# Expert weights for each token fetched by broadcast transfers instead of a matmul, and weight preparation moved into neighbouring stages

## Chip, cores and metric

The kernel runs on one core of a Trainium2 chip. The metric is the device time of one execution in microseconds (us). The core has a matmul engine (PE, with its weight loads PEld shown apart), a vector engine (DVE), an activation engine (ACT), a general engine (POOL), a queue that issues transfers (SP) and 16 DMA engines behind it.

## What is computed

A residual stream x of 4 x 256 tokens by 256 channels goes through four pairs of an attention-like layer and a feed-forward layer, each added with a tanh gate. The change touches layer 0's feed-forward, a mixture of 64 experts of width 64 with 4 chosen per token, and two shared ones of width 256:

```
logits = flat @ router_w                      # 1024 tokens x 64 experts
comb   = softmax scores of the top 4, normed; zero for other experts
g, u   = silu(flat @ wg[e]), flat @ wu[e]
routed = sum over e of comb[:, e] * (g * u) @ wd[e]
shared = the same with swg, swu, swd, and no comb
```

After it come layer 1's attention over the context (l1x), layer 1's feed-forward with an attention of its own (l1f), layer 2 with a feed-forward on weights rounded to -1, 0 and 1 (the rounding needs the mean of |w| over each whole weight), and layer 3. Those later layers need the weights Wq, Wk, Wv, Wc, W_in, W_up, W_down and the two rounded ones turned, 128 x 128 block by block.

## The kernel before

Each engine runs its own program, and semaphores order them. The stretch that matters has five parts.

**Start.** Layer 0's attention and the router. DVE's `chosen(h)` makes the combination weights of 512 tokens (h is 0 or 1) into `ct2`, twice side by side (line 2060). PE turns them (line 731), ACT copies them as rounded high parts to `comb` (`combine_high`), and DVE's `combine_low` puts the rest into the lower 64 partitions (line 2068).

**Routed experts.** Two experts make a pair, so 128 hidden rows fill the partitions; 32 pairs are 8 turns of a hardware loop with four slots `wraw`. A unit u is one pair and one half of the tokens: 64 units. PE runs `up(u+1)` (12 matmuls of 128x512: gate, then up, each in three high/low products), then one matmul `pick` x `comb` (line 769) that spreads the pair's weights over the partitions into a bank, then `down(u)` (6 matmuls, line 778). ACT makes `sg` (silu), DVE `hu` (line 2104) and `hh = bank * hu` (line 2108), ACT `hhi`, DVE `hlo` (line 2096), and `down(u)` waits for `hlo`. POOL splits each pair's raw weights into high and low (`split`, lines 2701 and 2704), and copies `pick`. SP loads the pair four ahead as soon as POOL has freed its slot (five transfers, 384 KB, lines 562 and 564).

**Shared experts.** Four more pairs (8 units) without weights. SP loads the two layer-2 weights `l2_raw` just ahead of them.

**Preparation.** When the experts are done, ACT copies `yT`, PE turns it and DVE adds it to `xs` (line 2125). Only then SP loads `stage` 0 to 3 and `wo`; ACT takes the sums of |w| (line 1602), PE adds them up (line 822), DVE rounds in six passes (lines 2133 to 2135) and makes the statistics of `xs` (from line 1974); PE turns 36 groups of blocks (lines 834 and 836) and ACT copies them out (line 1520), after the rounding is done. A last product `wa` (line 843) ends it, and everybody waits for it.

**Attention A.** 24 groups in slots written out by hand. In the first slots (-3 to -1) the pipeline fills: ACT `norm` (line 1684), POOL parts, PE turns, DVE maxima, ACT `mT`, a small transfer `qT<-mT`, and from slot 0 on `by_key`.

Of the kernel before, what the change touches and what calls it, by code (L numbers as in the profile page):

```python
# [8 lines left out]
P = 128  # L9
ALU = mybir.AluOpType  # L10
# [15 lines left out]
R = 16  # L26
# [114 lines left out]
def maxima_landed(stream, s):  # L141
# [6 lines left out]
     "router_ps", "router_max", "router_exp", "comb", "comb_ps", "comb_high", "comb_low", "x_split"),  # L148
# [11 lines left out]
    ("",) * 24 + ("pick_ready", "weights_high", "weights_split", "downs_split", "gate_made", "up_made", "gate_used",  # L160
                  "hidden_full", "hidden_high", "hidden_made", "up_used", "weight_made", "hidden_used", "experts_out", "y_rows",
# [31 lines left out]
def flamingo(nc, I, out):  # L193
    with ExitStack() as ctx:
        sems, batch_sems = {}, []

# [22 lines left out]
        def sb(name, shape, dt=F32):  # L219
# [64 lines left out]
        comb = sb("comb", [P, TOKENS], FR)  # L284
        picks = sb("picks", [P, E // 2, P], BF16)
        pick = [sb(f"pick{k}", [P, P], FR) for k in range(2)]
# [16 lines left out]
        First = namedtuple("First", "c cT kvT kv xn xT oT tmp lg lb lr cb ct ct2 m8 bn mv ve rs least st")  # L303
# [4 lines left out]
                       ct=sb(f"ct0{h}", [P, T0, E]), ct2=sb(f"ct2{h}", [P, T0, 2, E]), m8=sb(f"m8{h}", [P, T0, 8]),  # L308
# [20 lines left out]
        top[0] = region  # L329
        top[0] += DC * TOKENS * 4  # L330
        stage = [sb(f"stage{k}", [P, 2048]) for k in range(4)]
        wo = sb("wo", [P, DC, D])
        after_prep = max(top[0], after_experts + 8192)
        top[0] = region
        tern = [sb(f"tern{k}", [P, 2048], BF16) for k in range(2)]
# [43 lines left out]
        rc = sb("rc", [P, 16])  # L379
        at_f = sb("at_f", [P, B, NT, D])  # L380

# [131 lines left out]
        FIRST_STAGES = len(PREP)  # L513
# [3 lines left out]
        PREPB += blocks_of(tern[1], D, F1, lambda ic, o, n: w2qT[:, ic, o:o + n])  # L517

# [18 lines left out]
        def _(sp):  # L537
# [53 lines left out]
            sp.wait_ge(once("picks"), 2)  # L591
# [6 lines left out]
            sp.wait_ge(once("hidden_used"), 2 * PAIRS + 4)  # L598
            sp.wait_ge(once("experts_out"), 2 * HALVES)
# [7 lines left out]
            stg = once("stage_rest_loaded")  # L607
# [54 lines left out]
        def _(pe):  # L662
# [61 lines left out]
            def turn_combine(h):  # L724

                t = first[h]
                pe.wait_ge(S("comb"), h + 1)
                if h > 0:
                    pe.wait_ge(S("comb_low"), h)
                for i in range(T0):  # L730
                    last = pe.transpose(bank[7][:, i * P:(i + 1) * P], t.ct2[:, i, :, :], ident[:, :])
                last.then_inc(S("comb_ps"), 1)
# [14 lines left out]
            def up(k, h, u, pair, shared=False):  # L747

                n = 3 * (2 * k + h)
# [42 lines left out]
            pe.wait_ge(S("comb_low"), HALVES)  # L792
# [11 lines left out]
            for u in range(2 * SLOTN):  # L804
                if u + 1 < 2 * SLOTN:
                    up((u + 1) // 2, (u + 1) % 2, T * 8 + u + 1, T * SLOTN + (u + 1) // 2, shared=True)
                down(u // 2, u % 2, T * 8 + u, T * SLOTN + u // 2, last_pair=u // 2 == SLOTN - 1)

# [11 lines left out]
            pe.wait_ge(once("xs_updated"), 4)  # L820
            pe.wait_ge(once("abs_sums"), 2)
            mm(bank[4][:, 0:2], ones[:, :], st[:, 0:2], start=True, stop=True).then_inc(once("abs_total"), 1)

            pe.wait_ge(once("stage_loaded"), 5 * 16)
            for g, (srcs, dst) in enumerate(PREP + PREPB):
                if g >= 4:
                    pe.wait_ge(once("prep_done"), g - 3)
                if g == FIRST_STAGES:
                    pe.wait_ge(once("stage_rest_loaded"), 3 * 16)
                if g == len(PREP):  # L830
                    pe.wait_ge(once("ternary"), 2)
                for j, src in enumerate(srcs):
                    if g < len(PREP):
                        last = pe.transpose(bank[g % 4][:, j * P:(j + 1) * P], src, ident[:, :])
                    else:
                        last = pe.transpose(bankb[g % 4][:, j * P:(j + 1) * P], src, identb[:, :])
                last.then_inc(once("prep_made"), 1)

            g = len(PREP + PREPB)
            pe.wait_ge(once("prep_done"), g - 3)  # L840
            for m in range(DC):
                for cc in range(DC):
                    last = mm(bank[g % 4][:, m * R:(m + 1) * R], wo[:, cc, m * P:(m + 1) * P], am[:, cc, :],
                              start=cc == 0, stop=cc == DC - 1)
            last.then_inc(once("wa_made"), 1)
            pe.wait_ge(once("prepared"), 1)
            pe.wait_ge(once("prep_done"), len(PREP + PREPB))
# [146 lines left out]
            def attention(stream):  # L994
# [111 lines left out]
                def by_key(s, k):  # L1106
# [4 lines left out]
                    if stream == "C" and n == 0:  # L1111
                        pe.wait_ge(S("l2_pre"), 16)
                    if k == 0:
# [113 lines left out]
                for sl in range(-3, S_ + (1 if stream == "A" else 3)):  # L1227
                    here = lambda what: standing_there(stream, what, sl)
                    for k in range(8):
# [47 lines left out]
                        for s in here("by_query"):  # L1277
# [240 lines left out]
        def _(act):  # L1518
# [42 lines left out]
            def combine_high(h):  # L1561

                act.wait_ge(S("comb_ps"), h + 1)
                copy(comb[:, T0 * P * h:T0 * P * (h + 1)], bank[7][:, :]).then_inc(S("comb_high"), 1)
# [16 lines left out]
            def gate(k, u):  # L1581
                n = 3 * k
# [7 lines left out]
            with act.Fori(0, PAIRS // SLOTN) as t:  # L1590
                for k in range(2 * SLOTN):
                    gate(k, t * 8 + k)
            act.wait_ge(once("batch_cleared"), 1)
# [5 lines left out]
            act.wait_ge(once("l2_loaded"), 2 * 16)  # L1599

            for k, scratch in enumerate((w1qT, w2qT)):
                act.activation(scratch[:, :, :].rearrange("p c f -> p (c f)"), l2_raw[k][:, :], ACT.Abs, accum_out=st[:, k:k + 1]).then_inc(once("abs_sums"), 1)
            for g, (srcs, dst) in enumerate(PREP + PREPB):
                if g == 0:
                    act.wait_ge(once("ternary"), 2)
                act.wait_ge(once("prep_made"), g + 1)
                src = (bank if g < len(PREP) else bankb)[g % 4]
                copy(dst, src[:, 0:len(srcs) * P], scale=0.25 if g < DC else 1.0).then_inc(once("prep_done"), 1)

# [58 lines left out]
            def attention(stream):  # L1668
# [55 lines left out]
                for sl in range(-3, S_ + (2 if stream == "A" else 3)):  # L1724
                    here = lambda what: standing_there(stream, what, sl)
                    for k in range(8):
                        for s in here("by_key"):
# [58 lines left out]
            act.wait_ge(once("prepared"), 1)  # L1786
# [1127 lines left out]
```

## Time and profile before

| what | us |
|---|---|
| median of 3 runs | 1261.07 (1260.91 to 1263.65) |
| the profiled execution | 1259.72 |
| its span in the profile | 1257.9 |
| routed experts, first to last unit | about 87 to 369 |
| shared experts | about 369 to 405 |
| preparation, until attention A's first `norm` | 405 to 435.6 |

The profile gives for each engine what it did and what ended its waits. PE's clock is granted in two levels, 1.00 (2.4 GHz) and 0.50 (1.2 GHz). A share of DMA is that of 16 engines' time.

### The profile page before, as it was taken

To read this page: it belongs to the slowest core of one execution; us is meant where nothing else is said; L and a number is where in the kernel's file an instruction comes from. 1 tells how busy PE (TensorE), PEld (TensorE's weight loads), DVE (VectorE), ACT (ScalarE), POOL (GpSimd) and SP (SyncE) were. 2 spreads that over 40 slices of the span, in tenths; PEclk is the share of its full clock that TensorE was granted. 3 is DMA by queue.
4 is the path that set the end of the run, shared out by engine and by line. 5 is a ranking of instruction groups with operands and counts; after the bars stand their busy time and mean duration, and the time that the engine had idled before them with its cause. 6 is when DMAs were issued, how large, how long until landed. Compare 5 with 4: busy or idle time off the path is not lost.

```text
span 1257.9 us, 18978 instructions
## 1 busy us (share of the span) xinstructions
PE 1044.5 (83%) x6622; PEld 667.9 (53%) x6625; DVE 742.0 (59%) x1684; ACT 524.7 (42%) x883; POOL 328.0 (26%) x626
## 2 busy tenths in 40 slices
PE   4369999999998688877988899991464878999997
PEld 2258888888887432333455435650322434566575
DVE  6875554444443577787565212479697674784743
ACT  1223233333333556565554430233473553544543
POOL 7023434343333456435343200001310300000000
PEclk9659999999999768999999899795686799999999
DMA  6101121111310400000000300002000000000000
GB/s 151 42 1 39 38 50 42 46 46 42 117 25 1 142 2 2 2 3 2 3 3 4 118 1 1 1 1 51 1 2 1 3 2 1 1 9 1 9 10 9
DMA packets 62444, 32.09 MB, mean 26 GB/s; under 512 B 47104, under 2 KB 61072, under 8 KB 62112
## 3 DMA queue, kind: packets, MB, share of 16 engines
q1 hardware_dynamic: 62368, 31.10, 9.3%
q8 instruction: 45, 0.74, 0.2%
q14 instruction: 31, 0.25, 0.1%
HBM read 29.64 MB, written 1.05 MB: 24 GB/s over the span
## 4 chain that ended last, share of the span: by engine, by line
PE 69%; DVE 21%; ACT 4%; issue 3%; POOL 1%; DMA 1%; SPq 0%; POOLq 0%; DVEq 0%; ACTq 0%; PEldq 0%
PE bank L762 16%; PE bank L778 8%; PE bank L874 4%; PE bank L1160 3%; DVE mx L2272 3%; PE bank L989 2%; PE bank L1341 2%; PE bank L957 2%; PE bank L1358 2%; PE bank L919 2%; PE bank L1343 2%; PE bank L1092 2%; PE bank L1140 2%; PE bank L1193 1%; DVE mxc L2272 1%
## 5 line engine op out<-in xcount | busy, mean ns | idle before, releaser
L2272 DVE TENSOR_REDUCE mx<-bank 128x2 f32<-128x512 f32 (+1 forms) x176 | 117.7, 689 | 71.0 <-PE bank L1092 35.1
L1708 ACT ACTIVATE prob<-bank 128x512 f32<-128x512 f32 x176 | 102.9, 597 | 89.3 <-PE bank L1140 62.1
L1520 ACT ACTIVATE hhi<-hh 128x512 fp32r<-128x512 f32 x72 | 45.5, 632 | 153.1 <-DVE hh L2108 140.4
L2104 DVE TENSOR_TENSOR hu<-bank,sg 128x512 f32<-128x512 f32 x64 | 44.3, 692 | 97.1 <-PE bank L762 97.1
L762 PE MATMUL bank<-xh,wh 128*128 128x512 f32 x288 | 91.6, 399 | 0.0
L762 PE MATMUL bank<-xh,wl 128*128 128x512 f32 x288 | 90.5, 395 | 0.0
L762 PE MATMUL bank<-xlo,wh 128*128 128x512 f32 x288 | 90.1, 394 | 0.0
L2096 DVE TENSOR_TENSOR hlo<-hh,hhi 128x512 fp32r<-128x512 f32 x72 | 57.2, 794 | 50.7 <-ACT hhi L1520 50.7
L2704 POOL TENSOR_TENSOR wl<-wraw,wh 128x512 fp32r<-128x512 f32 x72 | 80.6, 1119 | 13.0 <-POOL wh L2701 13.0
L1585 ACT ACTIVATE sg<-bank 128x512 f32<-128x512 f32 x72 | 43.1, 598 | 61.9 <-PE bank L762 61.9
L762 PEld LDWEIGHTS bank<-xh,wh 128*128 128x128 f32 x288 | 54.6, 190 | 13.3 <-issue 0.3
L762 PEld LDWEIGHTS bank<-xlo,wh 128*128 128x128 f32 x288 | 54.3, 188 | 13.4
L762 PEld LDWEIGHTS bank<-xh,wl 128*128 128x128 f32 x288 | 54.4, 189 | 12.4
L874 PE MATMUL bank<-mun,xT 128*128 128x512 f32 x128 | 59.2, 607 | 1.2 <-ACT xw L1520 1.1
L778 PE MATMUL bank<-hhi,wh 128*128 128x512 f32 x144 | 56.8, 394 | 0.9 <-DVE hlo L2096 0.9
L778 PE MATMUL bank<-hhi,wl 128*128 128x512 f32 x144 | 56.9, 395 | 0.0
L1092 PE MATMUL bank<-kTx,qT 48*128 48x256 bf16 x256 | 51.0, 308 | 6.3 <-DVE kTx L2236 5.6
L778 PE MATMUL bank<-hlo,wh 128*128 128x512 f32 x144 | 56.1, 390 | 0.0
L2701 POOL CAST wh<-wraw 128x512 fp32r<-128x512 f32 x72 | 37.7, 523 | 64.1 <-PE bank L762 44.4
L1140 PE MATMUL bank<-qT,kTx 51*128 51x512 bf16 x128 | 51.2, 419 | 2.5 <-ACT prob L1708 2.5
L1708 ACT ACTIVATE probc<-bank 128x512 f32<-128x512 f32 x64 | 36.8, 596 | 36.1 <-PE bank L1140 35.7
L2272 DVE TENSOR_REDUCE mxc<-bank 128x2 f32<-128x512 f32 x64 | 41.4, 686 | 15.9 <-PE bank L1092 14.5
(456 smaller groups left out, 2275.0 us busy)
## 6 DMA issues: line engine op xcount, KB each, us to landing
wraw<-in_L_ffn_wg_dram SPq DMA_DIRECT2D x64, 64.0 KB, 2.3
wraw<-in_L_ffn_wu_dram SPq DMA_DIRECT2D x64, 64.0 KB, 2.4
wraw<-in_L_ffn_wd_dram SPq DMA_DIRECT2D x32, 128.0 KB, 2.4
l_raw<-in_L_ffn_w_dram SPq DMA_DIRECT2D x2, 1024.0 KB, 6.8
mun<-in_L_ffn_mu_dram SPq DMA_DIRECT2D x1, 2048.0 KB, 7.6
xs<-in_x_dram SPq DMA_DIRECT2D x1, 1024.0 KB, 5.5
w1s<-in_L_ffn_W_dram SPq DMA_DIRECT2D x2, 512.0 KB, 7.7
stage<-in_L_ffn_W_in_base_dram SPq DMA_DIRECT2D x1, 1024.0 KB, 7.8
```

What stands on the lines that cost most here:

```text
L762: last = mm(bank[4 + (n + m) % 4][:, :], w[k % 2][:, m, cc * P:(cc + 1) * P], v[:, cc, tok], start=j == 0 and cc == 0, stop=j == 2 and cc ...
L778: last = mm(bank[2 * m + h][:, :], w[k % 2][:, 2, m * P:(m + 1) * P], v[h][:, :], start=False, stop=last_pair and j == 2, skip_group_check ...
L874: last = mm(bank[n % 2][:, :], xT3[b % 2][:, cc, i * P:(i + 1) * P], mun[:, cc, ch * 512:(ch + 1) * 512], start=cc == 0, stop=cc == 1)
L1092: last = mm(to[:, f * N:(f + 1) * N], t.qT[rows, s % 4, u, i * P:(i + 1) * P], key_operand(L, b, s, 8 * g + 2 * j + f, rows, slice(0, N)), ...
L1140: last = mm(to[:, :], key_operand(L, b, s, 8 * g + 2 * j, rows, slice(ti * P, (ti + 1) * P)), t.qT[rows, s % 4, u:u + 2, :], start=True, s ...
L1520: return act.activation(dst, src, ACT.Copy, scale=scale)
L1585: act.activation(sg[k % 2][:, :], bank[4 + n % 4][:, :], ACT.Silu).then_inc(once("gate_used"), 1)
L1708: act.activation(t.prob[k][:, :], bank[3 + n % 2][:, :], ACT.Exp).then_inc(S("probs"), 1)
L2096: tt(hlo[k % 2][:, :], hh[k % 2][:, :], hhi[k % 2][:, :].bitcast(F32), ALU.subtract)\
L2104: tt(hu[k % 2][:, :], bank[4 + (n + 1) % 4][:, :], sg[k % 2][:, :], ALU.mult).then_inc(once("up_used"), 1)
L2272: V.reduce_max(out_, bank[n % 3][:, :].rearrange("p (h t) -> p h t", h=heads), AX, negate=True)\
L2704: G.tensor_tensor(low[:, cols, :], wraw[k][:, cols, :], high[:, cols, :].bitcast(F32), ALU.subtract)\
```

## The change

The selection product is gone. `comb` is now a plain [64 experts, 1024 tokens] tile; SP writes it once to `comb_rows` in device memory, and for each pair reads its two rows back, each spread over 64 partitions, into one of two `spread` tiles of 512 KB. The next transfer into a tile is issued when both `hh` of the pair that used it are done. DVE reads `spread` instead of a bank. The stage loads are issued while the shared experts run (their tiles lie elsewhere now), the sums of |w| and the rounding are placed between the shared units, and of the 36 turned groups only 12 stay ahead of the attention; 24 and `wa` go into its slots -4, -2 and -1.

```diff
@@ SP @@
+            def spread_weights(k, pair):
+                W(spread[k % 2][:, :], comb_rows.rearrange("(q e) t -> q e t", e=2)[pair].unsqueeze(1).broadcast_to([2, F, TOKENS]))\
+                    .then_inc(once(f"weights_spread{k % 2}"), 16)
...
+            sp.wait_ge(S("comb_high"), HALVES)
+            W(comb_rows, comb[:, :]).then_inc(once("comb_kept"), 16)
+            sp.wait_ge(once("comb_kept"), 16)
+            for k in range(2):
+                spread_weights(k, k)
+            end_of_batch(sp)
             with sp.Fori(0, E // 2 // SLOTN - 1) as t:
                 for k in range(SLOTN):
                     sp.wait_ge(once("downs_split"), t * SLOTN + (k + 1))
                     load_experts(k, t * SLOTN + (SLOTN + k), None)
+                    sp.wait_ge(once("hidden_full"), t * (2 * SLOTN) + (2 * k + 2))
+                    spread_weights(k, t * SLOTN + (k + 2))
+            for k in range(2):
+                sp.wait_ge(once("hidden_full"), E - 2 * SLOTN + 2 * k + 2)
+                spread_weights(k, E // 2 - 2 + k)
...
-            sp.wait_ge(once("hidden_used"), 2 * PAIRS + 4)
-            sp.wait_ge(once("experts_out"), 2 * HALVES)
+            sp.wait_ge(once("batch_arrived"), 4)
@@ PE @@
-                pe.wait_ge(once("up_used"), u + 2)
-                if not shared:
-                    if h == 0:
-                        pe.wait_ge(once("pick_ready"), pair + 1)
-                    mm(bank[4 + (n + 2) % 4][:, :], pick[k % 2][:, :], comb[:, tok], start=True, stop=True)\
-                        .then_inc(once("weight_made"), 1)
...
+                if u == 1:
+                    pe.wait_ge(once("abs_sums"), 2)
+                    mm(bank[6][:, 0:2], ones[:, :], st[:, 0:2], start=True, stop=True).then_inc(once("abs_total"), 1)
+                    pe.wait_ge(once("abs_total"), 2)
...
+            for g in PREP_AT["first"]:
+                prepare(g)
...
+                        if stream == "A":
+                            for g in PREP_AT.get((sl, k), ()):
+                                prepare(g)
@@ ACT, shared units @@
+                    act.activation(tern[k][:, :], l2_raw[k][:, :], ACT.Abs, accum_out=st[:, k:k + 1]).then_inc(once("abs_sums"), 1)
@@ DVE @@
-                    dve.wait_ge(once("weight_made"), u + 1)
+                    dve.wait_ge(once(f"weights_spread{k // 2 % 2}"), t * 32 + (16 * (k // 4) + 16))
-                    tt(hh[k % 2][:, :], bank[4 + (n + 2) % 4][:, :], hu[k % 2][:, :], ALU.mult).then_inc(once("hidden_full"), 1)
+                    tt(hh[k % 2][:, :], spread[k // 2 % 2][:, k % 2 * 512:(k % 2 + 1) * 512], hu[k % 2][:, :], ALU.mult)\
+                        .then_inc(once("hidden_full"), 1)
...
+                if k == 1:
+                    dve.wait_ge(once("abs_total"), 1)
+                    step(ts(wdq[:, :], bank[6][:, 0:2], 1.0 / (F1 * D), 1e-5, ALU.mult, ALU.max))
...
+                if k >= 2:
+                    w = l2_raw[(k - 2) // 3][:, :]
+                    if k in (2, 5):
+                        step(ts(w, w, st[:, 2 + k // 5:3 + k // 5], -1.0, ALU.mult, ALU.max))
...
+        PREP_BANKS = (3, 4, 5)
+        PREP_AT = {"first": range(12), (-4, 0): range(12, 16)}
+        for n in range(8):
+            PREP_AT[-2, n] = range(16 + n, 17 + n)
+            PREP_AT[-1, n] = range(24 + 2 * n, 26 + 2 * n) if n < 6 else range(30 + n, 31 + n)
```

POOL no longer copies `pick`, and it clears its tiles for the attention without waiting for the experts' end. DVE makes one `ct` where it made `ct2` twice, and `combine_low` is gone.

## Rows read from the trace of the kernel before

**Rows 1.** Windows, routed units: PE, PEld, DVE, ACT, POOL busy, PE clock, DMA share, GB/s

```profile
94.00:366.00 272.00, 272.00 (x1176) 220.32 (x1176) 135.50 (x187) 85.17 (x132) 107.86 (x154) 1.00 0.20 51
```

**Rows 2.** Chain that ended last: start, us, what

```profile
96.51 2.78 PE bank L762 x12
...
369.31 2.78 PE bank L762 x12
373.71 2.79 PE bank L762 x12
...
398.75 2.80 PE bank L762 x12
```

**Rows 3.** Timeline of one routed unit: start, us, engine, line [idle before]

```profile
342.06 0.69 DVE L2108 TENSOR_TENSOR hh<-bank,hu 128x512 f32<-128x512 f32 x1
...
343.45 0.69 DVE L2096 TENSOR_TENSOR hlo<-hh,hhi 128x512 fp32r<-128x512 f32 x1 [0.70 <-ACT hhi L1520]
...
345.76 0.39 PE L778 MATMUL bank<-hhi,wh 128*128 128x512 f32 x1
```

**Rows 4.** DMA view of 103 to 111.5 us, one pair's expert loads

```profile
q1 hardware_dynamic: 1232, 0.39, 20.3%
```

**Rows 5.** DMA view of 1124 to 1129 us, one output transfer, 128 partitions; last: KB, landing

```profile
DMA packets 272, 0.26 MB, mean 52 GB/s; under 512 B 16, under 2 KB 272, under 8 KB 272
...
q1 hardware_dynamic: 272, 0.26, 15.4%
...
out_dram<-xs SPq DMA_DIRECT2D x1, 256.0 KB, 2.2
```

**Rows 6.** DMA view of 452.4 to 452.8 us, one `qT<-mT`

```profile
DMA packets 15, 0.01 MB, mean 15 GB/s; under 512 B 3, under 2 KB 15, under 8 KB 15
```

**Rows 7.** Windows in large loads (last two: DMA share, GB/s)

```profile
715.00:718.00 3.00, 3.00 (x10) 1.46 (x9) 0.00 (x0) 1.70 (x3) 2.69 (x1) 0.50 1.02 354
709.00:713.00 4.00, 0.77 (x8) 0.51 (x6) 0.86 (x4) 0.60 (x1) 0.00 (x0) 0.84 0.89 358
```

**Rows 8.** Timeline of the start

```profile
76.39 2.12 DVE L2060 TENSOR_TENSOR ct<-ct,st 128x256 f32<-128x256 f32 x2
...
86.20 0.60 ACT L1520 ACTIVATE comb<-bank 128x512 fp32r<-128x512 f32 x1 [4.67 <-PE bank L731]
...
92.67 0.69 DVE L2108 TENSOR_TENSOR hh<-bank,hu 128x512 f32<-128x512 f32 x1
```

**Rows 9.** Timeline of POOL's split of one pair's gate and up weights

```profile
359.06 0.61 POOL L2701 CAST wh<-wraw 128x512 fp32r<-128x512 f32 x1 [0.91 <-PE bank L762]
...
359.85 1.30 POOL L2704 TENSOR_TENSOR wl<-wraw,wh 128x512 fp32r<-128x512 f32 x1 [0.18 <-POOL wh L2701]
```

**Rows 10.** Timeline of the preparation

```profile
405.57 2.06 ACT L1520 ACTIVATE yT<-bank 128x512 f32<-128x512 f32 x4 [2.52 <-PE bank L778]
...
408.89 3.23 DVE L2125 SCALAR_TENSOR_TENSOR xs<-bank,gates,xs 128x512 f32<-128x512 f32 x4 [5.12 <-PE bank L814]
...
420.71 2.70 DVE L1974 BATCH_NORM_STATS2 bn<-xs 128x6 f32<-128x256 f32 x8
420.83 1.98 ACT L1520 ACTIVATE wqkvT<-bank 128x256 f32<-128x256 f32 x6 [9.42 <-DVE tern L2135]
...
426.55 0.17 DVE L1979 SCALAR_TENSOR_TENSOR nmx<-mvx,rsx 128x8 f32<-128x8 f32 x1
...
435.61 1.09 ACT L1684 ACTIVATE xn<-xs,nmx,rsx 128x256 f32<-128x256 f32 x2 [0.69 <-DVEq L2141]
```

**Rows 11.** Windows of the preparation's last 24 groups, and of attention A's fill

```profile
426.40:435.00 8.60, 7.81 (x68) 5.32 (x66) 0.50 (x3) 8.52 (x25) 0.00 (x0) 1.00 0.00 0
436.00:454.00 18.00, 11.81 (x72) 6.04 (x72) 9.55 (x16) 5.93 (x9) 12.62 (x41) 0.50 0.01 2
```

**Rows 12.** Windows around the end of the experts

```profile
406.00:408.00 2.00, 0.22 (x2) 0.25 (x3) 0.00 (x0) 2.00 (x5) 1.94 (x2) 0.98 0.00 0
408.00:410.00 2.00, 2.00 (x11) 2.00 (x10) 1.09 (x2) 2.00 (x3) 1.83 (x5) 0.50 0.41 133
```

More of the change, by code:

```diff
@@ L283, in flamingo @@
         xh = sb("xh", [P, DC, TOKENS], FR)
-        comb = sb("comb", [P, TOKENS], FR)
-        picks = sb("picks", [P, E // 2, P], BF16)
-        pick = [sb(f"pick{k}", [P, P], FR) for k in range(2)]
+        comb = sb("comb", [E, TOKENS])
+        spread = [sb(f"spread{k}", [P, TOKENS]) for k in range(2)]
+        top[0] += 1024
         SLOTN = 4
@@ L728, in turn_combine @@
                 if h > 0:
-                    pe.wait_ge(S("comb_low"), h)
+                    pe.wait_ge(S("comb_high"), h)
                 for i in range(T0):
-                    last = pe.transpose(bank[7][:, i * P:(i + 1) * P], t.ct2[:, i, :, :], ident[:, :])
+                    last = pe.transpose(bank[7][0:E, i * P:(i + 1) * P], t.ct[:, i, :], ident[:, :])
                 last.then_inc(S("comb_ps"), 1)
@@ L745, in _, with up @@
             turn_combine(1)
-            def up(k, h, u, pair, shared=False):
-                n = 3 * (2 * k + h)
+            def up(k, h, u, pair):
+                n = 2 * (2 * k + h)
                 tok = slice(h * 512, (h + 1) * 512)
@@ L816, in _ @@
                 last.then_inc(once("y_rows"), 1)
[L820 to L829, printed above, removed]
+            pe.wait_ge(once("stage_loaded"), 8 * 16)
@@ L830, in _, with prepare @@
+            def prepare(g):
+                if g == 0:
+                    pe.wait_ge(once("xs_updated"), 4)
+                if g >= len(PREP_BANKS):
+                    pe.wait_ge(once("prep_done"), g + 1 - len(PREP_BANKS))
                 if g == len(PREP):
                     pe.wait_ge(once("ternary"), 2)
-                for j, src in enumerate(srcs):
+                if g == len(PREP + PREPB):
+                    for m in range(DC):
+                        for cc in range(DC):
+                            last = mm(bank[prep_bank(g)][:, m * R:(m + 1) * R], wo[:, cc, m * P:(m + 1) * P], am[:, cc, :],
+                                      start=cc == 0, stop=cc == DC - 1)
+                    last.then_inc(once("wa_made"), 1)
+                    return
+                for j, src in enumerate((PREP + PREPB)[g][0]):
@@ L840, in _ @@
[L840 to L847, printed above, removed]
+            for g in PREP_AT["first"]:
+                prepare(g)
@@ L1226, in attention @@
                 inside = lambda s: 0 <= s < S_
-                for sl in range(-3, S_ + (1 if stream == "A" else 3)):
+                for sl in range(-4, S_ + (1 if stream == "A" else 3)):
                     here = lambda what: standing_there(stream, what, sl)
@@ L1563, in combine_high @@
                 act.wait_ge(S("comb_ps"), h + 1)
-                copy(comb[:, T0 * P * h:T0 * P * (h + 1)], bank[7][:, :]).then_inc(S("comb_high"), 1)
+                copy(comb[:, T0 * P * h:T0 * P * (h + 1)], bank[7][0:E, :]).then_inc(S("comb_high"), 1)
             tokens_turned(0, 1, (6, 7))
@@ L1597, in _, with prepared @@
                     copy(yT[:, m, h * 512:(h + 1) * 512], bank[2 * m + h][:, :]).then_inc(once("experts_out"), 1)
[L1599 to L1605, printed above, removed]
+            act.wait_ge(once("ternary"), 2)
+            def prepared(g):
+                srcs, dst = (PREP + PREPB)[g]
                 act.wait_ge(once("prep_made"), g + 1)
-                src = (bank if g < len(PREP) else bankb)[g % 4]
+                src = (bank if g < len(PREP) else bankb)[prep_bank(g)]
                 copy(dst, src[:, 0:len(srcs) * P], scale=0.25 if g < DC else 1.0).then_inc(once("prep_done"), 1)
+            for g in PREP_AT["first"]:
+                prepared(g)
             def x_turned(b):
@@ L2059, in chosen @@
                 step(V.reciprocal(t.st[:, 4:8], t.st[:, 0:4]))
-                step(*[tt(t.ct2[:, :, k, :], t.ct[:, :, :], t.st[:, 4:8].unsqueeze(2).broadcast_to([P, T0, E]), ALU.mult)
-                       for k in range(2)])
+                step(tt(t.ct[:, :, :], t.ct[:, :, :], t.st[:, 4:8].unsqueeze(2).broadcast_to([P, T0, E]), ALU.mult))
                 dve.sem_inc(S("comb"), 1)
-            def combine_low(h):
-                dve.wait_ge(S("comb_high"), h + 1)
-                low = comb[E:2 * E, T0 * P * h:T0 * P * (h + 1)]
-                tt(low, bank[7][E:2 * E, :], low.bitcast(F32), ALU.subtract).then_inc(S("comb_low"), 1)
             norm0(0)
```

101 lines of the change are left out of this document (50 added, 51 removed).

## The prediction, on record before the result was known

> **What bounds the kernel now.** I read the windows first, to see which engine is full where: over the routed experts PE is busy all 272 us, at full clock, while DVE has half of it and the others less [rows 1]. The chain of waits says the same: from 96.51 to 369.31 us it is nothing but PE, one block of twelve matmuls per unit, 62 units in 272.80 us, so 4.40 us a unit; the shared units, which have no selection product, come every (398.75 - 373.71) / 6 = 4.17 us [rows 2]. The timeline of one unit shows that nobody else is close: `hlo` ends at 344.14 and the `down` that needs it starts at 345.76, 1.6 us of slack [rows 3]. After the experts the chain leaves PE. ACT ends its `yT` copies at 407.63, makes its sums, and then stands idle for 9.42 us until DVE's rounding is through; the first of the 36 copies starts at 420.83 and attention A's first `norm` at 435.61 [rows 10]. So two things are for sale: 0.23 us in each routed unit, and the 30 us between the experts and the attention.
>
> **Routed units: what goes.** The product costs PE 4.40 - 4.17 = 0.226 us a unit. The last one stands in the block at 369.31, since that is still 4.40 us ahead of the next. From the unit at 96.51 to the one at 373.71 it is 63 times: 14.2 us off, if PE stays the bound [rows 2]. `hh` reads `spread` instead of a bank; `hlo` already has both sources outside the banks, at the same 0.69 us [rows 3]. POOL's `pick` copies go too, on an engine with slack.
>
> **Routed units: what comes.** For each pair a transfer of 512 KB must land before the pair's first `hh`. Tile k is free when pair q's two `hh` are done, and pair q+2 wants it three units later less the stretch from the start of `up` to `hh`: about 4.2 + 4.2 + 2.8 = 11 us. That is the price at which PE starts to wait. What does the transfer take? Two facts decide.
>
> First, one engine's speed. In the window at 709 us the 16 engines moved 1.43 MB in 0.89 x 4.00 x 16 = 57 engine-us: 25.1 GB/s per engine; at 715 us, in which broadcast rows of 4 KB were read, 1.06 MB in 49 engine-us: 21.7 [rows 7].
>
> Second, how many engines take part. The output transfer from 128 partitions has 256 packets of 1 KB and 16 records below 512 B, one closing record for each engine [rows 5]. A `qT<-mT`, which goes from 12 partitions to 3, has 12 packets of 512 B and only 3 closing records [rows 6]: it ran on 3 engines, the count of its smaller outermost dimension. The new transfer's source is [2 experts][64 copies][1024 tokens]; the copies have no step in memory and can't be merged with the experts, so its outermost dimension is 2. By the reading of rows 6 it runs on 2 engines. Each moves 262 KB: 10.4 us at 25.1 GB/s, 12.1 at 21.7. I take 10.4, as the other engines are idle meanwhile.
>
> On the page "DMA: Bandwidth & Descriptors" (rules for kernel authors) the Trainium skill says the same against this change: a leading zero-stride broadcast of c copies, or any outermost dimension below 16, "confines the whole DMA to at most c engines". Rows 6 agree, with 3 closing records for the side of 3. By that page's specification of some 27 GiB/s an engine, an estimate, the 262 KB would take 9 us rather than 10.4.
>
> These two engines also carry their sixteenth of the expert loads: 20.3% of 8.5 us = 1.7 us a pair [rows 4]. So the two engines are busy 10.4 + 1.7 = 12.1 us for each pair, against 8.35 us that PE needs. Then it is no longer a matter of slack: throughput binds, whatever the order. The tile is asked for again about 3.6 us after it has landed (`hh`, `hhi`, `hlo`, `hu` and the second `hh`, four steps of 0.69 on DVE and one of some 0.7 on ACT, [rows 3]), while the other tile's transfer is still running, so that the queue of these two engines never empties. The forecast is one pair every 12.1 us.
>
> **Start.** `comb` is ready at 86.8 us [rows 8]. One of two `ct2` products in each half goes (1.06 of the 2.12 us that the first pair took), and PE's second turn no longer stands behind `combine_low(0)`; I take 1.4 us earlier in all, 85.4 (0.5 to 2). The write of 256 KB has the shape of the output transfer, 2.2 us [rows 5], so 87.6. Of those 2.2, 0.8 (15.4% of 5 us) are its packets and 1.4 the rest. The first spread lands at 87.6 + 1.4 + 10.4 = 99.4 (the first `hh` was at 92.67), the second at 109.8. 28 pairs follow with a load beside them, and two without: 109.8 + 28 x 12.1 + 2 x 10.4 = 469.4 for pair 31.
>
> **Into the shared units.** SP issues the 2 MB of `l2_raw` and the first shared load behind the last spread. On the two engines they come after it: 131 KB each, 5.2 us, and 1.7; then 1.4 of landing and 2.1 for POOL's split (0.61, a gap and 1.30, [rows 9]). The first shared `up` starts at 469.4 + 10.4 = 479.8. Without this wait PE would be there at 469.4 + 3.6; the wait costs 6. The next unit is at 484.0 and was at 373.71: 110.3 later. ACT's sums lie under that wait. The rounding takes DVE one pass of 1.2 to 1.4 us a unit, in some 2 us of idle time; I count nothing (0 to 1). At the second shared unit PE stops for a tiny product and DVE's answer: I estimate 0.9 us from small DVE steps of 0.17 [rows 10] and three hand-overs (0.5 to 1.5). Sum at the experts' end: +111.2.
>
> **Preparation.** It starts with the loads landed, the rounding done, and POOL ready. What is left ahead of `norm`: DVE's statistics, 6.0 us (420.71 to 426.72) from 412.12, so 418.2; and 12 groups, which took ACT from 420.83 to 426.4, 5.6 us [rows 10, 11], up to 8 if PE is at half clock. I take 419.3 against 435.61: 16.3 us off. The other 24 groups were 8.52 us of ACT and 7.81 us of PE at full clock; they go into a fill of 18 us in which ACT was busy 5.93 and PE 11.81 at half clock [rows 11]. Twice 7.81 and 11.81 is 27, 9 more than the fill; at full clock it is 1.6 more. In slot -1 eight groups stand ahead of ACT's `mT`, which the first `by_key` waits for. I take 5 (1 to 9). Net -11.3, bounds -15 to -7.
>
> **Sum.** 1257.9 + 111.2 - 11.3 = 1357.8 of span; the profiled execution took 1.8 more than its span and the median 1.35 more than that: 1361, and I say 1360.
>
> **Rivals.**
> *A: all 16 engines take part* (chance 0.12). For it: every large transfer of this trace did so; the only evidence for fewer is of small transfers between partitions, none from device memory. Then 512 KB are some 1.3 us of packets, landing in about 3, far below 11; the first `hh` comes near the old time (I take 0.6 us earlier). 1257.9 - 0.6 - 14.2 + 0.9 - 11.3 = 1232.7, some 1236 by the median. It decides at about 3 engines: with 4 the pair's load on an engine is 5.2 + 1.7 = 6.9, below 8.35, and the kernel is faster.
> *B: two engines, and the clock falls besides* (0.04). PE idles 3.7 us a pair. After the experts PE was nearly idle for two microseconds, and the clock went from 0.98 to 0.50 [rows 12]. At half clock a pair's matmuls take up to 16.7 us. If half of the pairs' time goes that way, a pair takes about 14.4 and the kernel 1361 + 30 x 2.3 = 1430. Against it: 1.5 us a pair are to spare before PE's work sets the pace again, and a short drop fits in.
> *C: two engines, but a pair costs less*, since the loads' packets slip between those of the spread or if one engine alone is faster than any window here shows (0.02): 10.4 a pair, 1361 - 28 x 1.7 = 1313.
> That nothing changes (0.02) would need errors that cancel.
>
> **How the numbers follow.** 0.80 for the forecast in its bounds: a pair from 11.2 us (half of the loads hidden) to 13.2 (the speed two thirds of the way to 21.7 GB/s) is 30 x -0.9 to 30 x +1.1 around 1361, 1334 to 1394, and the fill adds 4 on either side: 1330 to 1398. A, B and C are outside. Slower: forecast, B, C, 0.86. This kernel's measurement can tell 0.2%, or 2.5 us, from no change: same 0.02, faster 0.12.
>
> **What would show it.** In the profile after, the DMA view of one spread should have 128 packets of 4 KB and 2 closing records, and its landing some 12 us or more; `hh` should be released by `spread`'s DMA; the chain should step in pairs of 12 us with DMA in it; the DMA share in that stretch about 0.3 in spite of full queues. If instead there are 16 closing records, A is right and all from "routed units: what comes" to the shared wait falls. `norm` of attention A should follow the `xs` update by some 7 us instead of 23. Wrong would make me: an engine that reads 4 KB rows much faster or slower when alone, or a fill that swallows the groups or stalls on each.

## Result: 7% slower, and the profile after

The changed kernel takes 1349.6 us (median of 4 runs, 1347.46 to 1351.17), the kernel before 1262.4 in the same comparison: a ratio of 1.070, with an interval of 1.067 to 1.072. The forecast was 1360 in a range of 1330 to 1398.

| what | before | after |
|---|---|---|
| span of the profiled execution | 1257.9 | 1349.4 |
| first `hh` | 92.67 | 98.61 |
| first `hh` of the shared units | 372.19 | 470.13 |
| `yT`, the experts' end | 405.57 | 504.34 |
| attention A's first `norm` | 435.61 | 516.50 |
| attention A's first `prob` | 454.71 | 546.91 |

Read down, the difference is 5.9 us at the first `hh`, 97.9 at the end of the routed experts, 98.8 at `yT`, 80.9 at `norm`, 92.2 at `prob`, and 91.5 at the end. So the whole loss is made in the 32 pairs, where (470.13 - 98.61) / 32 = 11.61 us pass per pair. The last of these 32 steps is longer than the others, since it holds the stop ahead of the shared units: 14.14 us, from pair 31's first `hh` at 455.99, where the 31 steps before it take 11.53 us each. The new preparation takes 17.9 us off ahead of `norm`, and the fill of the attention's pipeline gives 11.3 of them back.

The windows show the routed stretch and the fill (columns as in [rows 1]):

```profile
100.00:450.00 350.00, 285.19 (x1088) 221.01 (x1089) 139.68 (x184) 80.49 (x129) 100.73 (x118) 0.91 0.25 79
516.50:546.90 30.40, 25.76 (x147) 14.05 (x145) 12.55 (x19) 15.96 (x34) 13.33 (x44) 0.59 0.00 1
```

PE, full before, is now idle for 65 of 350 us. The DMA share is 0.25, so three quarters of the 16 engines' time is free while everybody waits for transfers. What they wait for is in the view of waits (waiter <- releaser: us in total, times, longest):

```profile
DVE hh L2136 <- DMA spread<-comb_rows: 105.6, 32, 10.8
...
PE bank L799 <- DVE hlo L2124: 77.3, 31, 10.9
```

Once per pair `hh` waits for its spread, and PE for `hlo` behind it. The DMA view from 88 to 96 us, between the first spread's issue and its landing, shows how many engines carry it:

```profile
DMA packets 102, 0.42 MB, mean 52 GB/s; under 512 B 0, under 2 KB 0, under 8 KB 102
...
q1 hardware_dynamic: 102, 0.42, 12.7%
```

Nothing but packets of 4 KB, and 12.7% of 16 engines is 2.03 engines: two are busy all the time, at 26 GB/s each, and fourteen do nothing. The loads of the next experts were issued meanwhile, and none of their packets runs in these 8 us. The timeline of SP tells why:

```profile
82.83 0.56 SPq L605 DMA_DIRECT2D comb_rows<-comb  x1
85.81 1.26 SPq L585 DMA_DIRECT2D spread<-comb_rows  x2
87.62 10.18 SPq L574 DMA_DIRECT2D wraw<-in_L_ffn_wg_dram  x2
```

The two spreads are issued in 1.26 us; the two small loads behind them take SP 10.18 us to issue. They are held while the two busy engines work through the spreads. Therefore the longest pieces that the chain of waits has in the loop, where one would look first, name SP and not the spread:

```profile
82.83 2.97 DMA comb_rows<-comb
87.62 7.82 SPq L574
123.51 5.14 SPq L576
169.94 5.08 SPq L576
```

From 100 to 450 us SP's issues hold over four fifths of the chain (54.2% on line 574, 24.9% on 576, 5.2% on 585), and the spreads' transfers 4.2%, all of it in one piece of 14.78 us at 418.54, near the loop's end. Whether SP is the cause or only where the cause shows is a question for an experiment (the run with ACT's queue, below).

### The profile page after: what moved, and what is told of

Its sections match the earlier page's. It is cut to its first block, busy times and chain, and to the rows that moved or that the text cites. A ratio compares the mean times of both kernels' runs of the same rounds, so it can differ in the third digit from the quotient of the medians.

```text
span 1349.4 us, 18872 instructions
## 1 busy us (share of the span) xinstructions
PE 1067.5 (79%) x6560; PEld 672.3 (50%) x6560; DVE 743.7 (55%) x1680; ACT 520.9 (39%) x882; POOL 310.8 (23%) x591
## 4 chain that ended last, share of the span: by engine, by line
PE 45%; SPq 25%; DVE 18%; issue 5%; ACT 3%; DMA 2%; POOL 2%; POOLq 0%; DVEq 0%; ACTq 0%; PEldq 0%
SPq L574 15%; SPq L576 6%; PE bank L896 4%; PE bank L1185 3%; PE bank L1114 2%; PE bank L1011 2%; PE bank L1369 2%; PE bank L979 2%; PE bank L1386 2%; PE bank L941 2%; DVE mx L2302 2%; PE bank L1371 2%; PE bank L1165 2%; PE bank L790 1%; SPq L585 1%
## 5 line engine op out<-in xcount | busy, mean ns | idle before, releaser
L799 PE MATMUL bank<-hhi,wh 128*128 128x512 f32 x144 | 64.7, 449 | 77.3 <-DVE hlo L2124 77.3
L2136 DVE TENSOR_TENSOR hh<-spread,hu 128x512 f32<-128x512 f32 x64 | 50.7, 793 | 106.7 <-DMA spread<-comb_rows 105.6
L790 PE MATMUL bank<-xh,wh 128*128 128x512 f32 x288 | 99.7, 430 | 5.1 <-POOL wl L2728 4.8
L790 PE MATMUL bank<-xlo,wh 128*128 128x512 f32 x288 | 95.6, 415 | 0.0
L790 PE MATMUL bank<-xh,wl 128*128 128x512 f32 x288 | 94.0, 408 | 0.0
L799 PEld LDWEIGHTS bank<-hhi,wh 128*128 128x128 f32 x144 | 28.6, 199 | 96.2 <-DVE hlo L2124 62.6
L790 PEld LDWEIGHTS bank<-xh,wh 128*128 128x128 f32 x288 | 60.0, 209 | 20.7 <-POOL wl L2728 5.2
L790 PEld LDWEIGHTS bank<-xlo,wh 128*128 128x128 f32 x288 | 59.0, 205 | 15.0
L799 PE MATMUL bank<-hlo,wh 128*128 128x512 f32 x144 | 61.7, 428 | 0.0
L799 PE MATMUL bank<-hhi,wl 128*128 128x512 f32 x144 | 61.1, 424 | 0.0
```

What stands on the lines that cost most here:

```text
L790: last = mm(bank[4 + (n + m) % 4][:, :], w[k % 2][:, m, cc * P:(cc + 1) * P], v[:, cc, tok], start=j == 0 and cc == 0, stop=j == 2 and cc ...
L799: last = mm(bank[2 * m + h][:, :], w[k % 2][:, 2, m * P:(m + 1) * P], v[h][:, :], start=False, stop=last_pair and j == 2, skip_group_check ...
L2136: tt(hh[k % 2][:, :], spread[k // 2 % 2][:, k % 2 * 512:(k % 2 + 1) * 512], hu[k % 2][:, :], ALU.mult)\
```

## Experiments

### The same bytes on 16 engines, and on 4

The edit that matters most changes neither bytes nor rows, only the shape of the source. One transfer per expert, so that its outermost dimension is the 64 copies:

```diff
-                W(spread[k % 2][:, :], comb_rows.rearrange("(q e) t -> q e t", e=2)[pair].unsqueeze(1).broadcast_to([2, F, TOKENS]))\
-                    .then_inc(once(f"weights_spread{k % 2}"), 16)
+                for e in range(2):
+                    W(spread[k % 2][e * F:(e + 1) * F, :],
+                      comb_rows.rearrange("(q e) t -> q e t", e=2)[pair, e:e + 1, :].broadcast_to([F, TOKENS]))\
+                        .then_inc(once(f"weights_spread{k % 2}"), 16)
...
-                    dve.wait_ge(once(f"weights_spread{k // 2 % 2}"), t * 32 + (16 * (k // 4) + 16))
+                    dve.wait_ge(once(f"weights_spread{k // 2 % 2}"), t * 64 + (32 * (k // 4) + 32))
```

> Changed: the changed kernel, with each pair's spread transfer issued as two, one for each expert. The source of each is 64 copies of one row, so its outermost dimension is 64 where it was 2; bytes, rows and addresses are the same. Theory (two engines carry each spread, and their throughput sets the pair): all 16 engines take part, 33 KB each, and PE bounds the routed experts again: a pair every 8.4 us, no wait of hh for spread after the first, a median near 1262.4 - 0.6 - 14.2 + 0.8 - 6.6 = 1242 us (start, selection products, rounding beside the shared units, and what the new preparation took off by the trace of the changed kernel). Rival 1 (512 KB a pair, or 64 reads of the same row of device memory, is too much whatever engines carry it): pairs of about 11.6 us and 1350 us, as in the changed kernel. Rival 2 (what delays is SP, which issues the next transfer only when the queue has taken the last one): SP issues more now, 7 where it issued 6 per pair, and the median stays above 1300 us.

Measured: 1234.5 us (1230.3 to 1239.2), ratio to before 0.980 (0.976 to 0.984), so 115 us less than the changed kernel and faster than the kernel before. The window of its routed pairs:

```profile
100.00:350.00 250.00, 250.00 (x1080) 202.32 (x1079) 148.62 (x180) 82.99 (x127) 99.95 (x118) 1.00 0.45 113
```

PE is busy all 250 us at full clock. Its first `hh` starts at 90.40 and the first one of the shared units at 359.30: 8.40 us a pair. The waits and the DMA view from 200 to 233.6 us (last two columns: KB, us from issue to landing):

```profile
  DMA spread<-comb_rows: 3.0, 1
```

```profile
spread<-comb_rows SPq DMA_DIRECT2D x8, 256.0 KB, 3.9
```

One wait of 3.0 us, for the very first spread, and 3.9 us from issue to landing. Both rivals fall: neither the bytes nor the repeated reads of one row are too much, and SP issues one transfer more per pair without harm.

The second edit keeps the rows twice in device memory and leaves one transfer per pair, with a source of four rows of 32 copies:

```diff
-        comb_rows = nc.dram_tensor("comb_rows", (E, TOKENS), F32).ap()
+        comb_rows = nc.dram_tensor("comb_rows", (E, 2, TOKENS), F32).ap()
...
-                W(spread[k % 2][:, :], comb_rows.rearrange("(q e) t -> q e t", e=2)[pair].unsqueeze(1).broadcast_to([2, F, TOKENS]))\
+                W(spread[k % 2][:, :],
+                  comb_rows.rearrange("(q e) c t -> q (e c) t", e=2)[pair].unsqueeze(1).broadcast_to([4, F // 2, TOKENS]))\
...
-            W(comb_rows, comb[:, :]).then_inc(once("comb_kept"), 16)
-            sp.wait_ge(once("comb_kept"), 16)
+            for c in range(2):
+                W(comb_rows[:, c, :], comb[:, :]).then_inc(once("comb_kept"), 16)
+            sp.wait_ge(once("comb_kept"), 32)
```

> Changed: the changed kernel, with the rows kept twice in device memory (one more transfer of 256 KB at the start), so that the source of a spread is 4 rows of 32 copies each. Same bytes per pair, four engines where there were two. Theory (two engines' throughput): 131 KB an engine, 42 engine-us a pair over 4 engines is 5.3 us, with 1.1 us of expert loads 6.4 us, below the 8.35 us of PE: PE is the bound, and the time is within 3 us of that with 16 engines, some 1243 us. Rival (total bytes, or SP's issues): 1350 us, or somewhere between.

Measured: 1251.1 us (1245.7 to 1254.4), ratio 0.992 (0.988 to 0.995). (The 42 engine-us a pair in the expectation should read 21, a quarter of 84.3; its 5.3 us is worked out from 21.) In the loop the theory holds: 8.49 us a pair, and only the first `hh` waits for a spread. But the total is 17 us above the run with 16 engines, not 3. The two profiled executions are 19.9 us apart, and their traces say where: the first `hh` is at 100.14 in place of 90.40, the last pair's step takes 11.37 us in place of 8.43, since PE waits for the first shared weights, and the fill of attention A, from the first `norm` to the first `prob`, takes 30.8 us in place of 22.8. The first has two parts. `comb` was finished 3.8 us later, in a stretch that the edit does not touch. Then comes the chain's

```profile
86.91 3.63 DMA comb_rows<-comb
90.56 9.56 DMA spread<-comb_rows
```

where the run with 16 engines had 2.98 and 4.36, another 5.9 us. The fill is PE's clock, which two more windows show, first those with four engines, then with 16:

```profile
418.40:449.20 30.80, 25.78 (x139) 14.27 (x140) 12.77 (x20) 15.94 (x34) 13.29 (x44) 0.55 0.00 1
```

```profile
404.90:427.70 22.80, 16.95 (x139) 10.40 (x140) 12.67 (x20) 15.56 (x33) 13.05 (x43) 0.93 0.01 2
```

The same 139 matmul records, a granted clock of 0.55 against 0.93, 8.8 us more of PE's time and 8.0 us more of everybody's. In the expectation I had counted the fill as a constant; it has two values.

### Less in each spread, still on two engines

```diff
-                W(spread[k % 2][:, :], comb_rows.rearrange("(q e) t -> q e t", e=2)[pair].unsqueeze(1).broadcast_to([2, F, TOKENS]))\
+                W(spread[k % 2][:, 0:768], comb_rows.rearrange("(q e) t -> q e t", e=2)[pair, :, 0:768].unsqueeze(1).broadcast_to([2, F, 768]))\
...
-                    tt(hh[k % 2][:, :], spread[k // 2 % 2][:, k % 2 * 512:(k % 2 + 1) * 512], hu[k % 2][:, :], ALU.mult)\
+                    tt(hh[k % 2][:, :], spread[k // 2 % 2][:, k % 2 * 256:k % 2 * 256 + 512], hu[k % 2][:, :], ALU.mult)\
```

> Changed: the changed kernel, with only 768 of the 1024 tokens in each spread (packets of 3 KB for 4 KB, still two engines); the second half of the tokens is multiplied by the weights of tokens 256 to 767, so the output is that of other weights. Theory (two engines' throughput, near its threshold): 84.3 engine-us in four pairs is 10.5 us a pair and engine, three quarters are 7.9, with 1.0 to 1.7 us of expert loads 8.9 to 9.6 us a pair, still just above PE: 1350 - 31 x (11.57 - 9.25) = 1278 us, 1268 to 1288. Rival (a transfer costs by packet, not by byte: 128 packets as before): little less than 1350. Rival (latency of a chain from hh to the next spread, not throughput, sets the pair): a gain of 2.6 us a pair at most, and hh still waits for spread with the two engines idle for a part of each pair.

Measured: 1275.4 us (1274.0 to 1281.4). A pair takes (396.35 - 99.43) / 32 = 9.28 us, and its waits have the same form as with full spreads, at half the size:

```profile
DVE hh L2136 <- DMA spread<-comb_rows: 50.1, 29, 7.5
```

The second dose has 512 tokens (`0:512` in all four places, and both halves of the tokens read the same columns):

> Changed: the changed kernel, with only 512 of the 1024 tokens in each spread (packets of 2 KB, two engines); both halves of the tokens are multiplied by the weights of tokens 0 to 511, so the output is that of other weights. With 1024 tokens a pair took 11.61 us (hh of unit 0 to hh of unit 64, by 32), with 768 of them 9.28, so 2.33 us a quarter. Theory (throughput, below its threshold): 11.61 - 2 x 2.33 = 6.95 us an engine, less than PE's 8.35: PE is the bound, hh waits for spread only at the start, 8.4 to 8.5 us a pair as with 4 and 16 engines, and a median of 1235 to 1252 us, which that run's clock at the start and in the fill decides. Rival (the expert loads behind the spreads come late even so): hh, or PE by its weights, still waits in each pair, and the time lies at 1255 to 1275.

Measured: 1242.6 us (1238.9 to 1247.4), and (366.29 - 96.52) / 32 = 8.43 us a pair:

```profile
100.00:350.00 250.00, 250.00 (x1072) 202.19 (x1072) 146.77 (x178) 82.32 (x126) 99.81 (x118) 0.99 0.28 77
```

PE is full. Side by side, with KB (of 1000 bytes) for each of the engines that take part, and the pair once over all 32 steps and once over the 31 ahead of the last:

| tokens, engines | KB an engine | us a pair, 32 steps | 31 steps | median us |
|---|---|---|---|---|
| 1024, 2 | 262 | 11.61 | 11.53 | 1349.6 |
| 768, 2 | 197 | 9.28 | 9.12 | 1275.4 |
| 512, 2 | 131 | 8.43 | 8.39 | 1242.6 |
| 1024, 4 | 131 | 8.49 | 8.39 | 1251.1 |
| 1024, 16 | 33 | 8.40 | 8.40 | 1234.5 |

From 262 to 197 KB the pair follows the bytes, 2.41 us for 65.5 KB, which is 27 GB/s; below, it rests on PE. Rows three and four have the same bytes per engine and the same pair, although one moves twice as many bytes in all. The threshold lies between 131 and 197 KB an engine; the prediction put it at about 3 engines, which is 175 KB.

### Is SP the cause?

The spreads from pair 2 on go to ACT's queue, and SP has nothing but the loads of the experts in the loop:

```diff
-                    sp.wait_ge(once("hidden_full"), t * (2 * SLOTN) + (2 * k + 2))
-                    spread_weights(k, t * SLOTN + (k + 2))
...
+            act.wait_ge(once("comb_kept"), 16)
+            with act.Fori(0, E // 2 // SLOTN - 1) as t:
                 for k in range(2 * SLOTN):
                     gate(k, t * 8 + k)
+                    if k % 2 == 1:
+                        spread_weights(k // 2, t * SLOTN + (k // 2 + 2))
+            for k in range(2 * SLOTN):
+                gate(k, E - 2 * SLOTN + k)
+                if k in (1, 3):
+                    spread_weights(k // 2, E // 2 - 2 + k // 2)
```

> Changed: the changed kernel, with the spread transfers from pair 2 on issued by ACT's own queue, right behind hhi of the pair that used the tile, where SP issued them. SP's queue has the expert loads alone. The transfers themselves are as before, two outermost rows of 64 copies. Theory (the throughput of two DMA engines): the chain of waits named SP (21% of the span in its issues of expert loads), but SP was held up only because the queue behind it was full of spreads; without it a pair still takes 11.3 to 11.6 us and the median stays at 1340 to 1352 us. Rival (the blocked issues on SP are a cost of their own, since the next spread stands behind them): with the queue free of them a pair falls to the 10.5 us that a spread occupies an engine, or below, and the median to 1315 us or less.

Measured: 1349.8 us (1347.7 to 1353.0), ratio 1.070 like the changed kernel's, and (468.69 - 99.99) / 32 = 11.52 us a pair. The rival falls: the next spread no longer stands behind the loads' issues, and the pair stays as long. `hh` still waits for the spread, and one blocked issue can be seen on the new queue, the first of its 30 (the others took 0.54 us at most):

```profile
103.92 5.70 ACTq L1612 DMA_DIRECT2D spread<-comb_rows  x1
```

SP's share in the chain was where the two engines' backlog surfaced, not a cost of its own. One part of the expectation is wrong, though: SP was not held up only by spreads in its own queue. With none in it from pair 2 on, a load's issue between 100 and 345 us still takes 2.14 us on average, against 1.95 in the changed kernel and 0.58 with 16 engines, and lines 574 and 576 still have 15.5% and 4.4% of the whole chain. What these issues share with the spreads is the two busy engines.

### The preparation alone

The transfers' part is undone (product, `picks` and `combine_low` are back; in the shared units the banks go by two a unit), and the preparation's part stays:

```diff
-                    dve.wait_ge(once(f"weights_spread{k // 2 % 2}"), t * 32 + (16 * (k // 4) + 16))
+                    dve.wait_ge(once("weight_made"), u + 1)
...
-                    tt(hh[k % 2][:, :], spread[k // 2 % 2][:, k % 2 * 512:(k % 2 + 1) * 512], hu[k % 2][:, :], ALU.mult)\
+                    tt(hh[k % 2][:, :], bank[4 + (n + 2) % 4][:, :], hu[k % 2][:, :], ALU.mult)\
```

> Changed: the part on the preparation alone. The selection product, its picks and the low part of comb are as in the kernel before; the stage loads, sums, rounding and the 36 groups are where the changed kernel has them. Theory (sum of the changed kernel's own trace: 17.75 us off until the first norm, 11.2 us given back by the pipeline's fill with 24 groups and wa in it, 0.8 us in the shared units): 1262.4 - 17.75 + 11.2 + 0.8 = 1256.6 us, 1253 to 1259. Rival (the fill costs no more than the 5 us that was forecast, and the rest of the 11.2 us comes from the late transfers): 1250 us. Rival (the preparation saves nothing once the experts aren't delayed, since the stage loads then come later against them): 1262.

Measured: 1247.7 us (1247.6 to 1252.5), ratio 0.992 (0.989 to 0.995), 11.3 us faster than before where I expected 5.8. Its `norm` is at 418.15, 17.5 us earlier, as expected. The difference is the fill, 22.8 us where the changed kernel had 30.4. Here it is, and below it that of the kernel before:

```profile
418.15:440.98 22.83, 16.98 (x139) 10.44 (x140) 12.67 (x20) 15.58 (x34) 13.11 (x44) 0.93 0.01 1
```

```profile
435.60:454.70 19.10, 12.45 (x75) 6.18 (x76) 10.25 (x17) 6.79 (x9) 12.62 (x41) 0.50 0.01 2
```

Again a granted clock of 0.93 and the same 139 records. Against the 19.1 us of before, which ran at a clock of 0.50, the changed fill costs 3.7 us at the high clock and 11.3 at the low one. So the 3.7 is a net figure: the placement's cost, less what the faster clock gives back. The rival's 1250 is nearer than my sum, though its reason is not the one found: from `yT` to the first `prob` no engine waits for a transfer, here or there.

### Where the 24 groups stand

Both kernels below have 16 engines for the spreads. The first turns all 36 groups ahead of the attention:

```diff
-        PREP_AT = {"first": range(12), (-4, 0): range(12, 16)}
-        for n in range(8):
-            PREP_AT[-2, n] = range(16 + n, 17 + n)
-            PREP_AT[-1, n] = range(24 + 2 * n, 26 + 2 * n) if n < 6 else range(30 + n, 31 + n)
...
+        PREP_AT = {"first": range(36), (-1, 6): range(36, 37)}
```

> Changed: the changed kernel with each spread issued as two transfers (16 engines), and all 36 turned groups ahead of the attention; only the product wa stays in slot -1. The 24 groups cost ACT 4 x 0.51 + 8 x 0.33 + 4 x 0.54 + 8 x 0.33 = 9.5 us of copies ahead of norm, by the rows of the run with 16 engines, of which 0.8 us lies in ACT's idle time. Theory (the fill's price is 3.7 us where PE's granted clock is 1.00 in it, and 11.2 where it is 0.50): norm comes 8.7 us later and the fill is some 3 us shorter, so 5 to 6 us slower than 1234.5, 1240 us; if PE's clock comes out at 0.50 in the fill, that costs less here, since only wa is turned in it: 19 to 20 us from norm to the first prob, as in the kernel before, whatever the clock. Rival (the groups in the slots are what costs, full clock or not): as fast as 1234.5 us or faster.

Measured: 1239.9 us (1235.2 to 1243.9). `norm` comes 19.4 us after `yT`, where it came 11.8 after it; the fill takes 22.3 us at a clock of 0.55, more than the 19 to 20 that I gave it:

```profile
415.60:437.90 22.30, 14.82 (x86) 8.38 (x88) 11.51 (x19) 6.83 (x10) 13.22 (x44) 0.55 0.01 2
```

This fill has `wa` but none of the 24 groups, and is 3.2 us longer than that of before at nearly the same clock. So of the 11.3 us at the low clock some 8 go with the groups; where the other 3 come from no run shows. The interval of its ratio, 0.978 to 0.984, overlaps with that of the run with 16 engines, 0.976 to 0.984, so the 5 us between the medians are not settled. The second fills PE's idle time in slot -4:

```diff
-        PREP_AT = {"first": range(12), (-4, 0): range(12, 16)}
+        PREP_AT = {"first": range(13), (-4, 0): range(13, 20)}
         for n in range(8):
-            PREP_AT[-2, n] = range(16 + n, 17 + n)
-            PREP_AT[-1, n] = range(24 + 2 * n, 26 + 2 * n) if n < 6 else range(30 + n, 31 + n)
+            PREP_AT[-2, n] = range(20 + n, 21 + n)
+            PREP_AT[-1, n] = range(28 + 2 * n, 30 + 2 * n) if n < 2 else range(30 + n, 31 + n)
```

> Changed: the changed kernel with each spread issued as two transfers (16 engines), and the turned groups placed where PE had idle time: 13 ahead of the attention (12 before), 7 in slot -4 (4 before), 8 in slot -2, 8 in slot -1 (12 before). In the run with 16 engines PE is idle for 5 of the 6 us from 406.6 to 412.6, and then full until the first prob at 427.74. Theory (in the fill PE bounds): the four groups moved out of slots -2 and -1 take 4 x 0.33 us at full clock off, 1.3 us, less what the copies hold back qT; 1232 to 1234 us where the fill runs at full clock, and twice that gain at half clock. Rival (ACT's copies in slot -4 hold back qT and with it the whole fill): 0 to 2 us slower, 1235 to 1237.

Measured: 1234.3 us (1226.7 to 1235.5, 6 runs), ratio 0.976 (0.973 to 0.979). It is the fastest kernel here, but not by more than the measurement can tell from the one with 16 engines and the placement as changed. Its profiled run had the low clock through most of the fill:

```profile
401.60:428.70 27.10, 23.51 (x139) 12.65 (x138) 12.76 (x20) 15.68 (x33) 13.25 (x44) 0.62 0.01 1
```

27.1 us, against 30.4 to 30.8 in the two kernels above whose fill was at 0.55 to 0.59. The placement helps by some 3.5 us there, though part of that is the slightly higher clock. At full clock this fill was not seen.

## Why the prediction was right, step by step

**Two engines.** Right, and it decided the case. The evidence was two counts of closing records in small transfers [rows 5, 6]; after, 12.7% of 16 engines was busy and nothing else. That is what the Trainium skill, "DMA: Bandwidth & Descriptors" (rules for kernel authors), says of a broadcast behind an outermost dimension below 16; the trace agrees with 2.03 engines, and the run with the copies outermost agrees from the other side. The 2 closing records that I wanted to see are there, by count. The view of 200 to 246.3 us, four pairs, has

```profile
DMA packets 5446, 3.66 MB, mean 79 GB/s; under 512 B 4424, under 2 KB 4936, under 8 KB 5446
```

Four pairs' loads are 4 x 1232 = 4928 records [rows 4], all under 2 KB. The 8 that are left are 2 for each spread. With four engines the same count (200 to 233.6 us) is 4944, so 4 for each spread.

**The rate.** I took 25.1 GB/s from loads at nearly full DMA [rows 7]; the two engines moved 0.42 MB in 8 us, 26 GB/s each. The bound of 21.7 did not come near.

**12.1 us a pair.** It was 11.53 over 31 steps, 11.61 over all 32 (11.52 over 32 with ACT's queue). From 200 to 246.3 us, four pairs, the spreads' packets take 84.3 engine-us, so 10.5 us a pair on each of two engines, and all loads together 25.6 a pair, 1.6 on each of 16. Their sum is 12.1, the forecast, but the pairs take 0.5 less. So the terms were right and their plain addition was not. The records of that window show a part of the reason: more than two packets of 4 KB are open at once for 1.7 of the 46.3 us, so on one of the two engines they overlap, which is worth 0.2 us a pair. The rest of the 0.5 stays open, since the records do not say which load packets ran on these two engines. With 768 tokens the same sum is 8.2 + 1.6 = 9.8 against 9.12 measured, a larger gap. Pair 31's first `hh` came at 455.99 where I had 469.4; 12.6 of these 13.4 us are the shorter pairs, the largest error of the sum.

**Start.** The first `hh` was forecast for 99.4 and came at 98.61. Errors cancel in it: `comb` was ready at 82.8, not 85.4, but its write took 3.0 us for 2.2, and the first `hh` came 12.8 us after the spread's issue, for 11.8. Among the eight profiles with the plain `comb`, the start of its last copy lies near 82 us in three and at 83.9 to 85.8 in five: 4 us of spread in a stretch that the experiments don't touch.

**The shared units' wait.** Forecast 6 us (the recorded times give 479.8 - 469.4 - 3.6 = 6.8); PE was idle for 4.8 us ahead of the first shared `up`, since POOL's `wl` came late. That `up` then ran at a granted clock of 0.50 and took 5.49 us where 2.78 is usual, which the forecast did not have. The stop for the sums and the rounding between the units cost 0.8 us in all from the second `up` to `yT`, forecast 0.9.

**The preparation.** `norm` followed the `xs` update by 6.5 us, as forecast (7), and 17.9 us were saved ahead of it (16.3 forecast). **The fill** is the term that was mis-sized: 5 us (1 to 9) forecast, 11.3 measured. Its working had both cases: at full clock 1.6 us, at half clock 9. The 1.6 was put together wrongly, since it adds the groups at full clock to a fill whose 11.81 us of PE were read at half clock. And I took a value between the two cases, but the clock is one or the other. The runs show 3.7 and 11.3 for the changed placement, both against a fill at half clock.

**Net.** Where the sum had +110.3 us, at the second shared `up`, the trace has +98.0 (471.70 against 373.71); the preparation then took 6.6 off where it should have been 11.3. The sum came out 8.4 us high (span 1357.8 against 1349.4).

**The rivals.** A, all 16 engines, was not what the change did, but its sum was a forecast of the kernel that does it: a span of 1232.7, and the run with 16 engines measured 1232.7, its median 1234.5 against 1236. The match to a tenth is luck, as a start some 2 us earlier and a fill at high clock stand in it. "It decides at about 3 engines" is borne out by the doses: at 197 KB an engine the pair is still longer than PE needs, at 131 it is not. B (the clock falls in the loop) took little: it was 0.91 in the loop. C, 10.4 us a pair, had the right direction; the pair came out 0.6 us below the forecast, a third of C's 1.7.

## What to carry to other kernels

A broadcast from device memory should have its many copies outermost in the source. The same 512 KB kept two engines busy for 10.5 us; as two transfers with 64 copies outermost they landed 3.9 us after their issue, and by that alone the kernel went from 7% slower to 2% faster. Where the DMA share is low and everybody waits for transfers, count the engines (share times 16 in a window with one transfer) before looking at sizes or queues; here the queue that blocked in its issues was the place where it showed, not the cause. Price work that is moved into a pipeline's fill at both clock levels, take the fill's own time at the same level, and say which one the sum uses.

## What the runs showed that I had not expected

**Issues are held up for as long as a transfer.** Two issues behind two spreads took SP 10.18 us, and one on ACT's queue 5.70, in front of ACT's own work. With 16 engines the same two loads took 1.37 us to issue.

**The clock in the fill.** Seven profiles have the changed placement of the groups. PE was at 1.00 in all of them from the second shared unit to the experts' end, and fell to 0.50 (1.2 GHz) within the 20 us behind it; in the 4 us ahead of each fall it had been busy for 1.0 to 2.2. In two of them (16 engines, preparation alone) the first fall came 15.3 to 15.4 us after `yT` began, lasted 3.4 us, and the clock was at 1.00 (2.4 GHz) from there to the end of the fill. In the other five the first fall came 2.3 to 7.4 us after `yT` began; the clock came back for some 7 to 10 us and then fell a second time, for 31 to 38 us, in which PE worked nearly without a break. So an early first fall and a slow fill go together in these seven. What makes the first fall come early or late stays open; no run varied the idle time alone.

**DVE's `hlo` slows beside POOL's `wl`.** `hlo` takes 0.69 us by itself. Between 100 and 340 us of the run with 16 engines it took 1.01 to 1.28 us all 58 times that the trace has it, and all 58 times a `wl` of POOL runs at the same time, such as

```profile
202.01 0.74 POOL L2730 TENSOR_TENSOR wl<-wraw,wh 128x256 fp32r<-128x256 f32 x1 [0.18 <-POOL wh L2727]
202.03 1.28 DVE L2126 TENSOR_TENSOR hlo<-hh,hhi 128x512 fp32r<-128x512 f32 x1 [0.70 <-ACT hhi L1550]
```

With `pick` in POOL's order the two meet for less long: in the kernel before, `hlo` takes 0.69 us beside 0.11 us of a `wl`, and 0.89 beside 0.36, in turn. Without `pick` they share 0.46 to 0.73 us in every unit. PE was full all the same, so it cost nothing: `down` had 1.6 us of slack [rows 3].
